# A graph-attention and mixture-of-experts layer on one core: order of the 40-row turns, of three bias loads and of the last expert's output

## What is computed

```python
x = x + _L0_gnn_ref(_layernorm(x, axis=-1), adj, L0_gnn_W, L0_gnn_a1, L0_gnn_a2)
x = x + _L0_ffn_ref(_layernorm(x, axis=-1)[None], Wr, br, W1, b1, W2, b2)[0]

# _L0_ffn_ref, N = 1354 tokens, E = 8 experts, C = N // E = 169
probs = softmax(x @ Wr + br);  gate = max(probs);  idx = argmax(probs)
pos = (cumsum(one_hot(idx)) * one_hot(idx)).astype(int32)      # place of a token in its expert, from 1
mask = one_hot(idx) * (pos < C)                                # an expert takes 168 tokens, the rest drop out
expert_in = gate * x, gathered by expert and place
h  = relu(expert_in @ W1[e] + b1[e])
eo = h @ W2[e] + b2[e]
out = gate * eo, scattered back to the tokens
```

## Time and profile before

| | us |
|---|---|
| median of 3 runs (lowest, highest) | 280.75 (277.67, 281.6) |
| the profiled execution | 277.47 |
| its span, first to last instruction | 275.7 |

### The profile page before, as it was taken

How to read it: one execution, slowest core, us unless ns; L and a number is a source line. 1 busy time by engine, 2 the same in 40 slices (tenths; PEclk the granted TensorE clock), 3 DMA queues, 4 the chain that set the end, 5 groups by cost and what they waited for, 6 DMA issues and landing times.

```text
span 275.7 us, 4554 instructions
## 1 busy us (share of the span) xinstructions
PE 261.2 (95%) x1637; PEld 214.2 (78%) x1637; DVE 181.2 (66%) x428; ACT 129.0 (47%) x263; POOL 82.3 (30%) x113
## 2 busy tenths in 40 slices
PE   7999989999999999999999999995799999999991
PEld 2699989988887887787788997985476968868770
DVE  4978588986798778767524847442483764946712
ACT  2747776746557656556531212423317245353330
POOL 4344870001243403112211421471523324212022
PEclk9999999999999999999999999999599999999997
DMA  7980000333688885212112121159838688784001
GB/s 202 370 272 23 2 4 0 103 101 101 184 267 251 251 253 185 106 39 76 40 38 77 40 88 35 60 140 338 303 95 306 224 278 248 253 303 166 0 7 41
DMA packets 19210, 40.47 MB, mean 147 GB/s; under 512 B 2810, under 2 KB 3130, under 8 KB 19188
## 3 DMA queue, kind: packets, MB, share of 16 engines
q1 hardware_dynamic: 16196, 34.17, 37.5%
q0 software_dynamic: 2176, 4.80, 5.6%
q10 hardware_dynamic: 816, 1.21, 1.3%
HBM read 32.93 MB, written 8.31 MB: 150 GB/s over the span
## 4 chain that ended last, share of the span: by engine, by line
PE 80%; DMA 6%; POOL 4%; DVE 3%; issue 3%; ACT 2%; POOLq 0%; SPq 0%; ACTq 0%; DVEq 0%
PE bank L1412 28%; PE bank L1676 10%; PE bank L1714 8%; PE bank L1350 5%; PE bank L1398 5%; PE bank L1726 4%; PE bank L1646 4%; PE bank L1427 3%; DMA prob<-in_L_ffn_b_dram 3%; DMA x_all<-in_x_dram 2%; PE bank L1332 2%; PE bank L1439 2%; PE bank L1450 1%; PE bank L1546 1%; DMA vecs<-x_rows,src 1%
## 5 line engine op out<-in xcount | busy, mean ns | idle before, releaser
L1412 PE MATMUL bank<-h_hi,pt_lo 128*128 128x512 f32 (+1 forms) x110 | 45.9, 417 | 0.0
L1412 PE MATMUL bank<-h_lo,pt_hi 128*128 128x512 f32 (+1 forms) x110 | 43.6, 396 | 0.0
L1412 PE MATMUL bank<-h_hi,pt_hi 128*128 128x512 f32 (+1 forms) x110 | 43.4, 394 | 0.0
L409 POOL TENSOR_TENSOR x_all<-x_all,w_raw 128x512 f32<-128x512 f32 x10 | 18.1, 1813 | 65.2 <-ACT w_raw L587 65.2
L1676 PE MATMUL bank<-prob,w 128*128 128x168 f32 x224 | 33.2, 306 | 0.0
L1676 PEld LDWEIGHTS bank<-prob,w 128*128 128x128 f32 x224 | 32.6, 189 | 0.7 <-issue 0.2
L752 ACT ACTIVATE adj_s<-bank,b_cols 128x168 f32<-128x168 f32 x28 | 11.3, 402 | 39.5 <-PE bank L1676 39.5
L1210 DVE TENSOR_TENSOR h_lo<-w,h_hi 128x1024 fp32r<-128x1024 f32 x14 | 16.5, 1221 | 12.5 <-ACT h_hi L721 12.5
L1412 PEld LDWEIGHTS bank<-h_hi,pt_hi 128*128 128x128 f32 (+1 forms) x110 | 20.7, 188 | 5.0
L1412 PEld LDWEIGHTS bank<-h_hi,pt_lo 128*128 128x128 f32 (+1 forms) x110 | 20.7, 188 | 3.8
L1412 PEld LDWEIGHTS bank<-h_lo,pt_hi 128*128 128x128 f32 (+1 forms) x110 | 20.8, 189 | 3.6
(11 more groups left out here) (196 smaller groups left out, 562.5 us busy)
## 6 DMA issues: line engine op xcount, KB each, us to landing
w<-in_L_ffn_W_dram SPq DMA_DIRECT2D x16, 1024.0 KB, 5.5
adj_s<-in_adj_dram SPq DMA_DIRECT2D x10, 677.0 KB, 5.0
x_rows<-x_all SPq DMA_DIRECT2D x10, 257.0 KB, 3.4
out_dram<-x_all SPq DMA_DIRECT2D x10, 256.0 KB
x_all<-in_x_dram SPq DMA_DIRECT2D x9, 256.0 KB, 5.7
prob<-in_L_ffn_b_dram SPq DMA_DIRECT2D x5, 256.0 KB, 5.9
w_raw<-in_L_gnn_W_dram ACTq DMA_DIRECT2D x4, 256.0 KB, 5.4
adj_s<-in_L_ffn_b_dram SPq DMA_DIRECT2D x2, 256.0 KB, 7.0
```

The lines of the kernel that those rows point to most:

```text
L409: pool.tensor_tensor(x_all[0:R, t, 0:D], x_all[0:R, t, 0:D], relu_s[0:R, :], ALU.add).then_inc(s_x1, 1)
L1412: ins = pe.matmul(o_ps[par][0:R, :], p[0:K, par, k, 0:R], h[0:K, k, :], start=(k == 0 and n == 0), stop=(k == NT - 1 and n == 2))
```

## The change

Six pieces of code change:

- **in_turn and turn_first (PE)**: the loops over the column chunk c and the row block j are exchanged. All four 128-row blocks are turned first, then all four 40-row blocks. turn_first's wait for `s_rl` moves with c = 2 of the first group.
- **SP**: b2 of experts 1, 2 and 3 is issued right behind the last attention stores, ahead of the wait for the gather of expert 2. From e = 4 on b2(e) is issued behind W2(e), where it stood ahead of it.
- **DVE**: `out_bias(1)` and `final_first` move from the front of the loop and of round 1 to behind `hid_low(1)`; prepare(2) so comes directly behind `eo_bias_high`.
- **last expert, PE**: the new `wide_last` writes the 128 x 512 result as two ranges of 256 columns into two banks, and signals each (`s_yl`, then `s_y`); both narrow halves stand between its two contraction halves.
- **last expert, DVE**: `final(7)` finishes the narrow part first, then each column range as it is signalled.
- **parts(e)**: the last expert's order is now (1, 0), narrow first, for DVE and for POOL's scatter.

```diff
--- before.py
+++ after.py
@@ -180,6 +180,7 @@
         gx_ps, hid_ps, eo_ps, y_ps = ((banks[0], banks[1]), (banks[2], banks[3]),
                                       (banks[4], banks[5]), (banks[6], banks[7]))
         ya_ps, yb_ps = (banks[6], banks[4]), (banks[7], banks[5])
+        yl_ps = (banks[4], banks[6])
 
 
         s_x = [sem(f"s_xin{t}") for t in range(NT)]
@@ -222,7 +223,7 @@
         s_hid, s_eo, s_y, s_fin = (sem(n) for n in ("s_hid", "s_eo", "s_y", "s_fin"))
         s_zero, s_gt0, s_gx0, s_hid2, s_hc = (
             sem("s_zero"), sem("s_gt0"), sem("s_gx0"), sem("s_hid2"), [sem("s_hc_act"), sem("s_hc_dve")])
-        s_w2hi, s_w2lo, s_hidlo, s_vb = (sem(n) for n in ("s_w2hi", "s_w2lo", "s_hidlo", "s_vb"))
+        s_w2hi, s_w2lo, s_hidlo, s_vb, s_yl = (sem(n) for n in ("s_w2hi", "s_w2lo", "s_hidlo", "s_vb", "s_yl"))
         s_b2 = [sem(f"s_b2_{i}") for i in range(3)]
         s_strip, s_lt = sem("s_strip"), sem("s_lt")
         s_ohi, s_rl, s_g0, s_sh2 = (sem(n) for n in ("s_ohi", "s_rl", "s_g0", "s_sh2"))
@@ -246,7 +247,7 @@
 
         def parts(e):
 
-            return (0, 1) if e in (0, E - 1) else (1, 0)
+            return (1, 0) if e else (0, 1)
 
         def hold(eng, sem_, value):
 
@@ -329,15 +330,16 @@
                 if 1 <= t <= 4:
                     (load_w1, load_w2)[(t - 1) % 2]((t - 1) // 2)
 
-            sp.wait_ge(s_x1g[2], 32)
             sp.wait_ge(s_prob, NT)
             sp.wait_ge(s_pt[2], NT)
+            for e in range(1, 4):
+                load_b2(e)
+            sp.wait_ge(s_x1g[2], 32)
             for e in range(2, E):
                 load_w1(e)
-                if e == 2:
-                    load_b2(1)
-                load_b2(e)
                 load_w2(e)
+                if e >= 4:
+                    load_b2(e)
 
             sp.wait_ge(s_end[0], 32 * (E // 2))
             sp.wait_ge(s_end[1], 32 * (E // 2))
@@ -1250,9 +1252,18 @@
 
                 par = e % 2
                 for n, j in enumerate(parts(e)):
-                    dve.wait_ge(s_y, e * 2 + n + 1)
+                    if j and e == E - 1:
+                        dve.wait_ge(s_y, e * 2 + 1)
+                    elif e < E - 1:
+                        dve.wait_ge(s_y, e * 2 + n + 1)
                     dve.wait_ge(s_vb, 2 * (e - 1) + j + 1)
-                    if j == 0:
+                    if j == 0 and e == E - 1:
+                        for i, (done, k) in enumerate(((s_yl, 1), (s_y, 2 * E))):
+                            v = x1_g[e][:, 0, i * H0:(i + 1) * H0]
+                            dve.wait_ge(done, k)
+                            ins = dve.scalar_tensor_tensor(v, yl_ps[i][:, 0:H0], gate_s[:, 0, e:e + 1], v, ALU.mult,
+                                                           ALU.add)
+                    elif j == 0:
                         v = x1_g[e][:, 0, 0:D]
                         ins = dve.scalar_tensor_tensor(v, ya_ps[par][:, :], gate_s[:, 0, e:e + 1], v, ALU.mult, ALU.add)
                     else:
@@ -1267,15 +1278,15 @@
             w2_low(1)
             prepare(1)
             eo_bias_high()
-            out_bias(1)
             for e in range(1, E):
-                if e == 1:
-                    final_first()
-                else:
+                if e > 1:
                     final(e - 1)
                 if e + 1 < E:
                     prepare(e + 1)
                 hid_low(e)
+                if e == 1:
+                    final_first()
+                    out_bias(1)
                 if e + 1 < E:
                     w2_low(e + 1)
                     out_bias(e + 1)
@@ -1526,11 +1537,11 @@
 
 
                 pe.wait_ge(s_xg, 2)
-                for c in range(c0, c1):
-                    if c == 2:
-                        pe.wait_ge(s_rl, 2)
-                    o = (c % 2) * CAP
-                    for j in range(2):
+                for j in range(2):
+                    for c in range(c0, c1):
+                        if j == 0 and c == 2:
+                            pe.wait_ge(s_rl, 2)
+                        o = (c % 2) * CAP
                         pe.matmul(gx0_ps[c // 2][:, o + j * P:o + j * P + S[j]],
                                   xg0[0:S[j], j, c * P:(c + 1) * P], ident[0:S[j], 0:S[j]],
                                   start=(c % 2 == 0 and j == 0), stop=False, is_transpose=True)
@@ -1640,9 +1651,9 @@
             def in_turn(e):
                 pe.wait_ge(s_xg, e * 2 + 2)
                 pe.wait_ge(s_gxt, e)
-                for c in range(KC):
-                    o = (c % 2) * CAP
-                    for j in range(2):
+                for j in range(2):
+                    for c in range(KC):
+                        o = (c % 2) * CAP
                         ins = pe.transpose(gx_ps[c // 2][:, o + j * P:o + j * P + S[j]],
                                            xg[0:S[j], e % 2, j, c * P:(c + 1) * P], ident[0:S[j], 0:S[j]])
                 ins.then_inc(s_gt, 1)
@@ -1716,6 +1727,22 @@
                 if q:
                     ins.then_inc(s_y, 1)
 
+            def wide_last(q):
+
+
+                e, par = E - 1, (E - 1) % 2
+                if q == 0:
+                    pe.wait_ge(s_fin, 2 * E - 2)
+                pe.wait_ge(s_w2lo, 2 * (e - 1) + q + 1)
+                pe.wait_ge(s_hidlo, 2 * (e - 1) + q + 1)
+                for i in range(2):
+                    for c in range(2 * q, 2 * q + 2):
+                        for n, (v, w) in enumerate(((hid_lo, w2_hi), (hid_hi, w2_lo), (hid_hi, w2_hi))):
+                            ins = pe.matmul(yl_ps[i][:, 0:H0], v[par][:, c, :], w[par][:, c, i * H0:(i + 1) * H0],
+                                            start=(c == 0 and n == 0), stop=(c == KC - 1 and n == 2))
+                    if q:
+                        ins.then_inc((s_yl, s_y)[i], 1)
+
             def narrow_part(e, q):
 
 
@@ -1735,15 +1762,16 @@
                 pe.wait_ge(s_w2[e % 2], landed(e, e % 2))
                 if e >= 2:
                     pe.wait_ge(s_fin, 2 * e - 2)
-                wide_part(e, 0)
                 if e < E - 1:
-                    narrow_part(e, 0)
-                    narrow_part(e, 1)
+                    wide_part(e, 0)
+                else:
+                    wide_last(0)
+                narrow_part(e, 0)
+                narrow_part(e, 1)
+                if e < E - 1:
                     wide_part(e, 1)
                 else:
-                    narrow_part(e, 0)
-                    wide_part(e, 1)
-                    narrow_part(e, 1)
+                    wide_last(1)
 
             first_layer_first()
             second_layer_first()
```

## The result

| | before | changed |
|---|---|---|
| median us (lowest, highest, runs) | 279.6 (277.67, 281.6, 4) | 270.12 (269.27, 271.06, 4) |
| the profiled execution | 277.47 | 270.8 |
| its span | 275.7 | 269.1 |

The ratio is 0.966, with a 95% interval from 0.957 to 0.975: faster by 3.4%. The forecast was 267.0 us, with a range from 263.5 to 271.0. The median lies inside the range, 3.1 us over the forecast.

The account below looks back on a forecast made before the run. PE's list was taken to bound the kernel, except around round 1's stall. 277.5 - 7.3 (stall) - 6.3 (turns) + 2.0 (new wait) - 0.3 (tail) = 265.6 us, taken as 267.0 for a median, range 263.5 to 271.0.

Parts of the forecast that it names:

- stall in round 1: Before in_turn(2): PE's 4.8 us wait goes, and 2.5 us of slow clock behind it, together 7.3 us.
- signs of being wrong: W2(2) landing outside 192.3 to 195.5, a turn not under 1.1 us, or SP's wait for expert 2's gather ending after 183.7.
- W2(2) no earlier: Rival: gathers and W1(3) fill b2's room; 4.2 us wait at in_turn(3), clock falls again, 270.3 us; chance 0.15.
- The turns: Grouped transposes in seven in_turns and turn_first: 0.93 us each instead of 1.72, 0.79 saved, 6.3 us in all.
- 40 rows cost what 128 rows do: Rival on PE's turns: each 40-row transpose costs 0.109 us like a 128-row one; 266.4 us by the sum; chance 0.10.
- the 40-row transposes are dear in themselves: Rival on PE's turns: alternation is not the cost, so only 0.47 us saved each; 268.2 us; chance 0.08.
- What is late next: in_turn(3) starts no earlier than 7.65 us after W2(2) lands, put at 193.3: a new PE wait of 2.0 us.
- The clock behind the new wait: After in_turn(3)'s wait the granted clock stays at 1.00; a rival with a 4.2 us wait brought 2.5 us back.
- SP and b2: Three early b2 behind the last attention store cost nothing; without that cover, 2.5 us in front of the gathers.
- the prediction's limit on turn_first: The first gather also needs the last store of rows, so gathers may gain some 0.5 us instead of 0.8.
- The room of later rounds: From round 2 on DVE's chain runs 1.2 us ahead of PE, waits for no DMA, and this room stays.
- The tail: Last expert: nothing on PE, POOL's last scatter starts 0.5 us earlier but carries 128 rows; 0.3 us off.

Follow-up runs that it names:

- dve_only: The kernel before with DVE's new order alone, b2 still sent behind the gather; 276.9 us, ratio 0.990.
- sp_only: The kernel before with SP's early b2 alone, DVE's order the old one; 275.4 us, ratio 0.985.
- best_pairs: best with in_turn by pairs: two 128-row blocks, two 40-row blocks, and the same again; 267.3 us, one run.
- best_alt: best with in_turn back in the old alternating order, turn_first still grouped; 270.7 us, ratio 0.961.
- best: Changed kernel; SP waits for expert 1's gather, prepare(3) ahead of w2_low(2), out_bias(2) behind hid_low(2); 264.9 us, ratio 0.950.
- tail_only: The kernel before with the last expert's new order alone (wide_last, final, parts); 283.6 us, one run.
- turns_only: The kernel before with the new loop order of in_turn and turn_first alone; 275.3 us, ratio 0.984.
- after_again: The changed kernel unaltered, measured once more beside best; 270.5 us, ratio 0.969.
- round1_only: The kernel before with early b2 and DVE's new order, without grouped turns or new tail; 274.5 us, ratio 0.982.
- prep3: The changed kernel with prepare(3) moved directly behind out_bias(1), ahead of w2_low(2); 266.9 us, ratio 0.956.
- w_early: The changed kernel without SP's wait for the gather of expert 2; 268.6 us, ratio 0.963.
- both: The changed kernel with the edits of prep3 and w_early together; 267.9 us, ratio 0.958.

## Why the prediction was right, point by point, and what it missed

The direction and the mechanism were right: the stall in round 1 went, the turns became shorter by the forecast amount, and a new wait came where it was said to come. The size was right only through the width of the range. The forecast had a range of its own, 264.5 to 269.5, and 270.1 lies outside it; the span is 5.3 us over the 263.8 of the sum. Two of the prediction's own signs of being wrong came up as well: W2(2) landed outside 192.3 to 195.5 (at 196.25), and SP's wait for the gather of expert 2 ended later than 183.7 (at 184.85). The rival "W2(2) no earlier" gave 270.3, nearest to the measured time, but its condition, a wait of 4.2 us, was not met: this is a coincidence of sums.

- **The stall in round 1** was right in place and size. in_turn(2) has no wait, its clock is at 1.00, and first_layer(2) starts 10.5 us behind in_turn(1)'s first layer (196.18 and 185.68) where it took 18.7: 8.2 us less, for 7.3 + 0.8 forecast. dve_only shows that DVE's order alone takes this wait away, and sp_only that early b2 alone leaves 1.8 us of it.
- **The turns** were right: 0.90 us for 0.93 forecast, 0.81 saved for 0.79. The 40-row blocks cost what the 74-row row had suggested, so the cases "40 rows cost what 128 rows do" and "the 40-row transposes are dear in themselves" fall: two of them in a row start 0.062 to 0.084 apart. The change between 128 and 40 rows is what costs, as best_pairs and best_alt show. By the Trainium skill's rule for weight loads ("TensorE: Matmul & The Clock Gate", "LDWEIGHTS (loading the stationary operand)") each of them would have a load of 0.107 for its 128 columns. The trace does not bear that out as a price per transpose: their starts are 0.062 and 0.063 apart at a granted clock of 1.00. The Trainium skill's "TensorEngine Tiling (Array Packing)", "Key Properties", states that a change of tiling mode drains the engine. The trace agrees in so far as a change between 128 and 40 rows costs 0.14 us and one between 128 and 74 nothing; no record of it says that the former is a change of tiling mode.
- **turn_first** saved its 0.80 (0.87 in the chain for 1.67), and counted in full, though in_turn(1) starts 1.1 us later than in the trace of before. From two transposes of the front at some 53 us (L1579, L1590 in the change) to in_turn(1) it is 129.2 to 129.3 us in the traces with the old turn_first and no fall of the clock (before, dve_only, sp_only), and 128.4 in those with the new one and no fall (best, best_pairs): 0.8 less. The fall at the end of the attention adds 1.5 or 1.6 us in every trace that has it and no wait at in_turn(1); the changed kernel has 130.0. No step of the prediction had such a fall, since the trace of before had none there. Another 0.4 us lie ahead of 53 us, where the changed kernel's trace is already later (53.74 and 53.35); what makes them stays open.
- **What is late next** was right as a mechanism to the tenth: 7.65 us from the landing of W2(2) to in_turn(3) forecast, 7.6 measured in four traces. Its input was the mis-sized term. The landing was put at 193.3; it came at 196.3. Some 1.9 of that is the late front, which moved PE too and so costs no wait. Of the other 1.0 most is the step "two b2 no longer stand ahead of it, at 319 GB/s 1.6 us": from SP's issue of W1(2) to the landing it took 12.3 us before and 11.4 after, 0.9 less in place of 1.6. Some 0.2 more is SP's go, which came 0.3 us earlier, the late front taken off, where 0.5 was forecast. So the wait was 3.0 instead of 2.0 us. The 12.3 us that the forecast started from were a quick case: with the two b2 in the queue dve_only and tail_only took 14.2 and 14.1. The 1.6 us by the mean rate may thus be right on average and wrong against this one trace.
- **The clock behind the new wait** was the second miss. The forecast kept it at 1.00 behind a wait of 2 us and let it fall only in the rival with 4.2. At 3.0 us it fell, and cost 2.44 + 2.57 - 1.58 - 1.86 = 1.6 us. That part of the outcome lies between the forecast and that rival.
- **SP and b2** were rightly put at next to nothing. The first gather starts 7.64 us behind the issue of the last store of rows, and 7.48 in turns_only, which sends no b2 there; both wait for that store, as the prediction's limit on turn_first has it. DVE waited for no b2.
- **The room of later rounds** did not quite stay. W2(5) landed 7.6 us after its issue, and PE waited 0.3 us at in_turn(6). That the landing stays as quick when rounds are 0.8 us shorter was not argued.
- **The tail** was worth 0.05 us, not 0.3. PE costs nothing, as forecast (5.2 us from the start of its wide part to its end, before and after). Counted from the start of that wide part, the last scatter starts 0.5 us earlier, also as forecast, but not for the reason given: in neither kernel does it wait for DVE's last piece; it follows POOL's first scatter directly, and that one starts 0.4 us earlier. Against it, the last scatter now carries 128 rows in place of 40, and from its start to the end of the span it takes 4.4 us instead of 4.0. The prediction named that load and put too small a price on it. Before (the second is in the earlier trace rows), then changed:

```profile
270.43 0.99 POOL L447 DMA_INDIRECT out_dram<-x_all,dest  x1 [5.72 <-DVE x_all L1257]
```

```profile
263.41 0.91 POOL L449 DMA_INDIRECT out_dram<-x_all,dest  x1 [4.83 <-DVE x_all L1272]
264.63 1.01 POOL L449 DMA_INDIRECT out_dram<-x_all,dest  x1 [0.30 <-issue]
```

- **The sum.** From in_turn(1) to the end it gave 93.1 - 7.3 - 5.5 + 2.0 - 0.3 = 82.0 us; it was 85.3. The 3.3 us are 1.0 of wait, 1.6 of clock, 0.3 in the later round, 0.25 of tail and 0.15 unexplained. The front is 1.9 us later than forecast: 1.5 are the fall of the clock, 0.4 lie ahead of it. The allowance of 1.4 us over the sum for a median was made for another reason than this; that it covers a part of the miss is luck.

In the traces the parts are worth less alone than together: early b2 alone and DVE's order alone each leave a wait of their own (2.4 and 0.5 us gained from the mark on, 5.6 with both), while the turns alone are partly lost in the wait of round 1 when it is long. The ratios of these kernels overlap, so the runs do not show it.

## What to carry to other kernels

When a wait is taken out of an in-order engine's list, follow the same list one round further: what stood behind the wait now waits for the next transfer, and its length is that landing plus all the work between. Moving the step that the critical engine needs ahead of the step that waits for the transfer disturbs nothing else, where hurrying the transfer made a gather late; and a wait that holds transfers back may protect an earlier gather. Group TensorE's transposes of 40 rows apart from those of 128: here 0.14 us went with each change taken out, six of them per turn. Between 74 and 128 rows no such price is seen, so look at the distances between starts first. And when a forecast starts from one trace, ask whether its transfers landed early or late for that kernel.

## What the runs showed of the hardware that was not expected

- The granted clock fell to 0.50 at 157 to 160 us, with PE at work without a gap before it, in 9 of the 14 profiled executions; it lasted 3.4 us each time, and the way from 53 us to in_turn(1) was 1.5 or 1.6 us longer with it, where no wait at in_turn(1) blurs it. Neither the change nor any edit is near it: before and tail_only have the same code there, and one had the fall and the other not.
- The fall behind a wait did not go by the wait's length alone: after 1.8 us (sp_only) the clock was at 0.50 for 6.8 us and after 2.7 us (after_again) for 3.4, while 1.5 and 1.6 us (round1_only, prep3), and also 1.8 and 2.4 us at in_turn(1) (w_early, both), had no fall behind them.
- One transfer in a full queue lands at very different times: b2(1), with the same transfers ahead of it, took 7.4 us in the profile of before, 9.4 in dve_only, 9.8 in turns_only and 10.5 in tail_only. A step that waits for such a landing brings this into the kernel's time. That the change makes the time steadier is not shown: its four first runs lie within 1.8 us and those of before within 3.9, but the six of after_again lie within 3.9 as well.
- A change between 128 and 40 contraction rows costs TensorE 0.14 us in these float32 transposes, one between 128 and 74 rows nothing. A scatter of 128 rows at the end takes 0.4 us longer to finish than one of 40.
